# Attention and convolution on one core: the max tiles from 64 rows, in pairs on the two row halves, around the prob x val matmuls

## What is computed

```python
t = _gn(x).reshape(B, C, S).transpose(0, 2, 1)            # S = 1024 positions
q, k, v = t @ Wq.T + bq, t @ Wk.T + bk, t @ Wv.T + bv
q, k, v = (z.reshape(B * NUM_HEADS, S, hd) for z in (q, k, v))   # 8 heads, hd = 64
attn = softmax(einsum('gqd,gkd->gqk', q, k) / sqrt(hd))
wv = einsum('gqk,gkd->gqd', attn, v).reshape(B, S, NUM_HEADS, hd).transpose(0, 2, 3, 1)
x = x + wv.reshape(B, C, W, H)
x = x + conv3x3(relu(_gn(x) * mask(_gn(x))), weight) + bias
```

## Time and profile before

| | |
|---|---|
| median of 3 runs | 2684.11 us (2684.02 to 2684.46) |
| the profiled execution, own time | 2683.13 us |
| its span in the trace | 2681.2 us |
| granted TensorE clock, mean | 0.989 |
| TensorE matmul busy | 2560.5 us, 95%, 11424 instructions |
| VectorE busy | 2030.5 us, 76% |
| ScalarE busy | 1088.5 us, 41% |
| GpSimd busy | 1110.8 us, 41% |
| max tiles on TensorE (L646) | 1024, 388.3 us busy |
| their reductions on VectorE (L1186) | 1024, 661.0 us busy, 684 ns each |
| prob x val (L693) | 2048 records, 499.8 us busy |

### The profile page before, as it was taken

How to read it: one execution, slowest core, us unless ns; L and a number is a source line. 1 busy time by engine, 2 the same in 40 slices (tenths; PEclk the granted TensorE clock), 3 DMA queues, 4 the chain that set the end, 5 groups by cost and what they waited for, 6 DMA issues and landing times.

```text
span 2681.2 us, 38876 instructions
## 1 busy us (share of the span) xinstructions
PE 2560.5 (95%) x11424; PEld 1004.8 (37%) x11424; DVE 2030.5 (76%) x2804; ACT 1088.5 (41%) x1801; POOL 1110.8 (41%) x881
## 2 busy tenths in 40 slices
PE   5999999999999999999999999976999999999998
PEld 2333333333333333333333333322344444444443
DVE  5887787787788788778878877787468968968614
ACT  3455455445545545544554554443322132122100
POOL 3356466546556646655655564534103003003000
PEclk9999999999999999999999999988999999999999
DMA  5224142241423414323243331521254653744534
GB/s 150 80 74 114 61 130 82 61 133 48 123 81 95 112 40 130 100 66 110 61 118 93 92 94 33 152 84 58 90 209 169 221 203 126 275 149 142 188 109 158
DMA packets 209768, 309.01 MB, mean 115 GB/s; under 512 B 80272, under 2 KB 129552, under 8 KB 209552
## 3 DMA queue, kind: packets, MB, share of 16 engines
q1 hardware_dynamic: 209552, 306.36, 37.0%
HBM read 202.88 MB, written 52.69 MB: 95 GB/s over the span
## 4 chain that ended last, share of the span: by engine, by line
PE 83%; DVE 11%; issue 3%; ACT 1%; POOL 1%; DMA 0%; DVEq 0%; SPq 0%; ACTq 0%
PE bank L786 28%; PE bank L693 15%; PE bank L671 13%; PE bank L628 11%; PE bank L646 7%; PE bank L638 5%; DVE nmax L1186 3%; PE bank L660 2%; DVE prob_sum L1180 2%; PE bank L687 1%; ACT prob L869 1%; DVE nt L219 1%; DVE rstd L224 1%; PE bank L654 1%; DVE nt L221 1%
## 5 line engine op out<-in xcount | busy, mean ns | idle before, releaser
L1186 DVE TENSOR_REDUCE nmax<-bank 128x1 f32<-128x512 f32 x1024 | 661.0, 684 | 227.3 <-PE bank L646 213.1
L869 ACT ACTIVATE prob<-bank 128x512 f32<-128x512 f32 x1024 | 556.0, 596 | 653.5 <-PE bank L671 647.2
L786 PE MATMUL bank<-v,u_slab 128*128 128x512 f16 x3456 | 746.9, 379 | 0.0
L1026 POOL TENSOR_TENSOR prob_sum<-prob_sum,prob 128x512 f32<-128x512 f32 x360 | 526.0, 1461 | 419.4 <-ACT prob L869 417.9
L693 PE MATMUL bank<-prob,val 128*64 128x512 f32 x2048 | 499.8, 606 | 0.0
L786 PEld LDWEIGHTS bank<-v,u_slab 128*128 128x128 f16 x3456 | 338.2, 98 | 406.9 <-issue 0.8
L646 PE MATMUL bank<-k_a,q_a 128*128 128x512 f16 x1024 | 388.3, 385 | 27.4 <-DVE nmax L1186 22.0
L1180 DVE TENSOR_TENSOR prob_sum<-prob_sum,prob 128x512 f32<-128x512 f32 x360 | 358.9, 997 | 12.0 <-DVE shift L1196 8.9
L671 PE MATMUL bank<-q_a,k_a 128*128 128x512 f16 x1024 | 315.4, 382 | 17.7 <-ACT prob L869 16.0
L671 PE MATMUL bank<-q_b,k_b 128*128 128x512 f16 x1024 | 306.0, 381 | 2.4 <-DMA q_b<-shift 2.2
L1077 POOL TENSOR_TENSOR t_a<-tab_mem 128x1224 f32<-128x1224 f32 x16 | 49.2, 3073 | 460.6 <-DVEq L1309 446.9
(11 more groups left out here) (124 smaller groups left out, 2647.9 us busy)
## 6 DMA issues: line engine op xcount, KB each, us to landing
u_slab<-u_scratch SPq DMA_DIRECT2D x72, 1024.0 KB, 5.0
tile<-x_scratch SPq DMA_DIRECT2D x34, 1024.0 KB, 7.2
xs<-x SPq DMA_DIRECT2D x28, 1024.0 KB, 5.7
u_scratch<-u_w SPq DMA_DIRECT2D x96, 192.0 KB, 2.7
q_a<-qk_hi SPq DMA_DIRECT2D x64, 256.0 KB, 4.8
den_sb<-recip_scratch SPq DMA_DIRECT2D x128, 128.0 KB, 2.9
x_scratch<-xr SPq DMA_DIRECT2D x16, 1024.0 KB, 4.3
xr<-x SPq DMA_DIRECT2D x15, 1024.0 KB, 8.0
```

What stands on the lines that cost most here:

```text
L786: mm = pe.matmul(bank_at(pos, co)[:].rearrange("p (i n) -> p i n", i=2), slab[:, l, c, co * P:(co + 1) * P], image[v][:, 2 * c:2 * c + 2, ...
L869: act.activation(prob[:, (2 * u + e) % 8], sc_bank[bank_turn(s * 16 + 2 * u + e, 16 * HPI)[0]][:], ACT.Exp, scale=float(D) ** -0.5).then_i ...
L1026: nc.gpsimd.tensor_tensor(acc, in0, prob[:, (2 * kc + 1) % 8], ALU.add).then_inc(s1["sum1"], 1)
L1186: dve.tensor_reduce(nmax[:, m // 2, m % 2:m % 2 + 1], src[:], AX.X, ALU.max, negate=True)\
```

## The change

Each max tile is now made from the high halves alone, with a contraction over 64 rows: the even tiles from rows 0 to 63 of q_a and k_a, the odd ones from rows 64 to 127 of q_a and k_b. For that k high is put on rows 64 to 127 of k_b, q low on those of q_b, and the shift row and its 8.0 row are row 0 of q_b and k_b. The product of q high and k low is no longer part of the maximum (it stays in the scores). The tiles come in pairs of an even and an odd one: `MAX_PAIRS` = [2, 1, 2, 1, 2, 0, 0, 0]. In units 0, 2 and 4 one pair stands behind score part 1 and one behind `weigh_pair` (a new place, "e"), in units 1 and 3 one pair between the score parts. Place "a" is gone.

```diff
-MAX_QUOTA = [2, 3, 3, 3, 3, 2, 0, 0]
+MAX_PAIRS = [2, 1, 2, 1, 2, 0, 0, 0]
...
-    first = sum(MAX_QUOTA[:u])
-    tiles = [("max", first + k) for k in range(MAX_QUOTA[u])] if nxt else []
-    at = {"a": tiles[0:1], "b": tiles[1:2], "c": tiles[2:]}
+    first = 2 * sum(MAX_PAIRS[:u])
+    tiles = [("max", first + k) for k in range(2 * MAX_PAIRS[u])] if nxt else []
+    at = {"b": tiles, "c": []} if u % 2 else {"b": [], "c": tiles[0:2], "e": tiles[2:]}
...
-                hi_to = ((k_a, 0), (k_b, 0)) if which == 0 else ((q_a, 0), (q_a, D))
-                lo_to = (k_a, D) if which == 0 else (q_b, 0)
+                hi_to = ((k_a, 0), (k_b, D)) if which == 0 else ((q_a, 0), (q_a, D))
+                lo_to = (k_a, D) if which == 0 else (q_b, D)
...
-                sp.dma_start(q_b[half][D:D + 1, :, tok], shift[:, s % 2]).then_inc(s1["shift_row"], 16)
+                sp.dma_start(q_b[half][0:1, :, tok], shift[:, s % 2]).then_inc(s1["shift_row"], 16)
...
-                pe.matmul(dst[:].rearrange("p (k t) -> p k t", t=TOK), q_a[half][:, m // 2, tok],
-                          k_a[half][:, 4 * (m % 2):4 * (m % 2) + 4, tok],
+                k_hi, row = ((k_a, slice(0, D)), (k_b, slice(D, P)))[m % 2]
+                pe.matmul(dst[:].rearrange("p (k t) -> p k t", t=TOK), q_a[half][row, m // 2, tok],
+                          k_hi[half][row, 4 * (m % 2):4 * (m % 2) + 4, tok],
...
-                    run("a")
                     scores(h, s, u, 0)
                     run("b")
...
                     if u >= 2 and u % 2 == 0:
                         weigh_pair(h, s, u // 2 - 1, den_direct(s, more))
+                    run("e")
...
-                nc.gpsimd.memset(k_b[half][D:P], 0.0).then_inc(s1["kb_clear"], 1)
-                nc.gpsimd.memset(q_b[half][D:P], 0.0).then_inc(s1["kb_clear"], 1)
+                nc.gpsimd.memset(k_b[half][0:D], 0.0).then_inc(s1["kb_clear"], 1)
+                nc.gpsimd.memset(q_b[half][0:D], 0.0).then_inc(s1["kb_clear"], 1)
...
-                nc.gpsimd.memset(k_b[half][D:D + 1], 8.0).then_inc(s1["kb_clear"], 1)
+                nc.gpsimd.memset(k_b[half][0:1], 8.0).then_inc(s1["kb_clear"], 1)
...
-                    for place in "abcd":
+                    for place in "bcde":
```

More of the change, by code:

```diff
@@ L711, in run @@
                     def run(place):
-                        for kind, a in items[place]:
+                        for kind, a in items.get(place, ()):
                             if kind == "max":
```

## The result

The changed kernel takes **2771.18 us** (median of 4 runs, 2769.24 to 2774.72), the kernel before 2684.28 us beside it: a ratio of 1.032, 95% interval 1.0305 to 1.0336. That is 87 us slower. The forecast was 2704 us, 20 us slower, with a range up to 2745: the sign is right, the size is not, and the time lies outside the range.

What follows compares the result with a forecast made beforehand. PE (TensorE) was taken to bound the attention phase, so every step counts in full. Terms -104 + 60 + 48 + 12 + 16 - 11 = +21 us on a median of 2684.1 gave 2704 us, range 2650 to 2745.

Steps and rivals of the forecast that it cites:

- Tiles: Max tiles on PE: sixteen steps of 0.216 us become eight if halves fully overlap, -1.73 us a slot, -104 us.
- No overlap: Rival: the two halves of a pair do not run together, each pair takes 0.43 us; 2782 us, chance 0.07.
- Changes of shape: PE switching array shape around max pairs: five visits a slot at 0.20 us each, +1.0 us a slot, +60 us.
- The ring: Three banks hold max tiles; PE waits 0.4 us at each pair between score parts, +0.8 us a slot, +48 us.
- slots 0 and 1: In unit 3, extra VectorE work delays the bank for the pair between score parts: +0.87 us in 14 slots, +12 us.
- C pairs: Pairs between the two score parts of odd units, two a slot; each saves 0.22 us, pays 0.20 and 0.4.
- Slots 3 and 7: Without projections, fewer max tiles cover PE's wait for exp between units: +0.43 us twice and +0.22, +16 us in all.
- Waits that go: PE waits in slot 6 vanish, -0.9 us in 7 slots; slot 2 is 0.65 us better 7 times; -11 us together.
- The same DMAs are issued, at the same places of SP's queue: DMAs of the new layout: only their target rows change, so they cost nothing.
- Slots 60 to 62 at nothing: Last image's three late slots that still make max tiles are paced by others than PE; the change costs nothing there.
- The rule of the Trainium skill that I set against the change: Tiling speeds TensorE up, not the emptying of PSUM; reductions stay at 0.69 us, their cost counted in the ring term.
- The estimate of 2735 us from the Trainium skill: A pair takes longer than one step: 1.3 steps for a set, 0.065 us a pair, making it 2735 us.

Runs made afterwards that it cites:

- run 6: Changed kernel with its 64-row max tiles standing singly in the order of the kernel before: 2816.66 us, ratio 1.049.
- run 5: Changed kernel with one VectorE instruction moved, the reciprocal of unit 4 ahead of the reductions of the pair behind prob x val: 2749.24 us, ratio 1.0243.
- run 7: Changed kernel with the pair between the score parts put behind the second part, and the reciprocal moved as in run 5: 2716.7 us, ratio 1.0114.
- run 8: run 7 with unit 0's first pair ahead of the first score part and VectorE's moments last in units 1 and 2: 2688.21 us, ratio 1.0017.
- run 4: Changed kernel with the shift made one unit earlier, in unit 5 instead of 6: 2776.07 us, ratio 1.0347.
- run 2: Changed kernel's order with max tiles over all 128 rows instead of 64: 2752.56 us, ratio 1.0263.
- run 9: run 8 with the next slot's shift issued behind prob x val of unit 6 in slots 3 and 7: 2678.51 us, ratio 0.9974.
- run 10: run 9 with, in slot 2 alone, the pair ahead of unit 0's first score part moved to unit 5: 2678.85 us, ratio 0.9981.
- run 3: Changed kernel with the pair between the score parts put behind the second score part: 2740.86 us, ratio 1.0211.

## Why the prediction went wrong, step by step

- **Tiles, -104 us: right.** The halves overlap; the pair costs one step. "No overlap" (2782 us) came within 11 us of the measured time and was still wrong: a time alone does not tell the cases apart.
- **Changes of shape, +60: right.** 0.10 us each, 0.20 a visit (runs 6 and after). The plain slot has +0.14 where -1.73 + 1.0 + 0.8 gives +0.07.
- **The ring, +48, and slots 0 and 1, +12: right in kind; the total is nearly right partly by luck.** The second tiles of 126 C pairs start 72.9 us in all behind the first, 0.58 each, against 60 us by the prediction. For the two pairs of a slot together (images 1 to 5) it is 0.81 us in slot 5, where 0.8 was taken, and 1.17 in slots 0 and 1, where 1.67 was; but 1.48, 1.54 and 1.59 in slots 3, 6 and 7, where 0.8 was.
- **Slots 3 and 7, +16: right.** The wait between score parts 0 grew from 0.52 to 1.39 us there (by starts, per slot), +0.87, where 2 x 0.43 was worked out. What these slots lost beyond that is the ring's, 0.7 to 0.8 us a slot more than was taken.
- **Waits that go, -11: wrong.** In slot 6 the wait ahead of the sums' matmuls went, and the C pairs wait 0.7 us more than a plain slot was given. In slot 2 more went than I had taken (17 us for 4.6), and the wait for the row took over.
- **"The same DMAs are issued, at the same places of SP's queue": this is the step that failed.** I costed the DMAs at nothing. Their places are the same, but a queue in program order is as late as its first member, and that hangs on a reciprocal on VectorE, which the new place "e" pushed behind two reductions. I had looked at PE's own waits and at what VectorE does for the ring, and asked of nothing else on VectorE who waits for it; nor had I asked what the two tiles ahead of score part 1 of unit 0 had covered. What the runs showed in its place: PE's list has 33.6 us more at the row and 6.8 at the loop's turns, and in slots 0 to 58 the lower clock was granted nine times for 3.4 us (in six of the eight slots 2 and three times in slot 1), where it was once before; at 1.66 us each that is some 13 us. The three make 53 us, but they are not 53 of the 67 us between forecast and result, since in slot 2 they stand where PE had waited for VectorE. Putting the one reciprocal back returned 22 us (run 5), and 28 more went with the cover and the moved moments (runs 7 and 8). Runs 5 and 4 show the chain; that the cover is the larger part of run 8 is not shown, since its two edits were not run apart.
- **"Slots 60 to 62 at nothing": wrong.** Together they went from 123.2 to 130.7 us, nearly all of it in slot 61 (40.1 to 48.4). It comes with the order and not with the halves: slot 61 takes 49.3 us in run 2, full tiles in the new order, and 39.9 in run 6, halved tiles in the old one. Even run 9 has 47.2 there. Which wait it is was not looked for and stays open.
- The rule of the Trainium skill that I set against the change (TensorEngine Tiling (Array Packing), PSUM Bottleneck) points to the ring: it holds in kind, since the reductions became no shorter (682 ns each, 684 before). The estimate of 2735 us from the Trainium skill (TensorE: Matmul & The Clock Gate, Measured speedup vs the span model) has no support: a pair takes one step.

The range failed because all its cases varied terms that I had found. None was kept for a wait that the old order had hidden.

What the halves give directly is seen only where nothing waits. The plain slot had no idle time before and next to none in run 9; it takes 29.23 us there against 29.79, -0.56, where the terms give -0.63 (-1.73 and 1.0, and 0.10 for the change of shape that place "a" adds). An image takes 223.9 us in run 9 against 226.1 before; but image 0 is 2.2 us longer, so slots 0 to 59 are 12.3 us shorter in all, and slots 60 to 62 take 5.8 of that back (129.0 against 123.2). Full tiles in the order of run 9 were not run, so how much of its gain over the kernel before is due to the other moves is not shown.

## What to carry to other kernels

When work is moved on an engine that runs in program order, list everything queued behind it there, small instructions too, and follow each to the queue it feeds: here a reciprocal of 0.19 us started a chain of DMAs with a row at its end that TensorE needs. When filler is moved away, ask what it had been covering. And a saving on the bottleneck counts only with the waits around it: in the order of the change halving the tiles made the kernel slower by 19 us, and with the halved tiles in a mended order it is 0.15 to 0.36% faster than before.

## What was not expected of the hardware

**Small VectorE instructions stand still beside GpSimd.** In runs 5 and 7 to 10 PE waits 1.8 to 2.8 us in each slot 2 for VectorE, at max tiles. The instructions shown are part of the statistics of the next image, 128 x 4 numbers each. Run 8, VectorE, then GpSimd in the same time:

```profile
1037.88 1.20 DVE L216 TENSOR_SCALAR rstd<-nt 128x4 int32<-128x4 int32 x1
1039.11 1.18 DVE L219 TENSOR_TENSOR nt<-rstd 128x4 f32<-128x4 f32 x1
...
1041.19 1.20 DVE L224 SCALAR_TENSOR_TENSOR rstd<-nt,rstd 128x4 f32<-128x4 f32 x1
1042.42 0.16 DVE L219 TENSOR_TENSOR nt<-rstd 128x4 f32<-128x4 f32 x1
```

```profile
1037.78 1.27 POOL L1027 TENSOR_TENSOR prob_sum<-prob_sum,prob 128x512 f32<-128x512 f32 x1
1039.00 1.27 POOL L1040 TENSOR_TENSOR xr<-xr,den_sb 128x512 f32<-128x512 f32 x1
...
1041.10 1.27 POOL L1027 TENSOR_TENSOR prob_sum<-prob_sum,prob 128x512 f32<-128x512 f32 x1
```

The same instruction takes 0.16 us when GpSimd is still and 0.83 to 1.20 when it is not; each slow one shown starts just behind a GpSimd instruction and ends just behind that one's end. The chain of five such instructions costs about 5 us instead of 1. In the changed kernel the same lines took 0.16 to 0.17 us (1079.08 to 1080.04), because the late broadcasts held GpSimd idle until 1081.04; from 1081.06 on they took 0.83 to 1.26 us there too. In the kernel before five of them had taken 0.84 to 1.20 us, from 1036.62 on, and PE its 19.2 us of waits in the slots 2. So the cure of the row's wait gave part of itself back: GpSimd got its work earlier and stood in VectorE's way again. The Trainium skill has the rule (SBUF — State Buffer, "SBUF: two separate sides": VectorE and GpSimd share a pair of ports, and whoever holds it blocks the other for its whole instruction; it holds for a VectorE instruction in a two-port mode, or with two inputs in SBUF beside a GpSimd one that reads SBUF). The rows agree in that VectorE's instruction of 1039.11 ended at 1040.29, 0.02 us behind GpSimd's of 1039.00; which mode VectorE ran in they do not show. No run moved GpSimd's work alone, so the cause rests on the two timelines.

**A short wait can cost more than its length.** Behind 2.26 us of idle time the granted clock was 0.52 for 3.4 us, and eight passes took 3.55 us instead of 1.89; behind 1.69 us in run 3, 3.45. But the length of the wait alone does not decide it. In the changed kernel eight passes took 1.94 us behind 2.56 us of idle time (slot 2 of image 5) and behind 0.99 us (slot 4). In run 4 even the longest wait for the row was followed by passes at their usual length:

```profile
1091.22 0.60 PE L672 MATMUL bank<-q_b,k_b 128*128 128x512 f16 x2 [3.56 <-DMA q_b<-shift]
...
1092.08 1.94 PE L694 MATMUL bank<-prob,val 128*64 128x512 f32 x8
```

**The loop's turn costs more when a load has just been issued.** From PE's last projection to its next matmul it took 1.11, 2.47 and 0.74 us before, after the change and in run 5 (means of five turns), where the load of 1 MB had been issued 6.2, 4.7 and 7.1 us ahead of that projection. That it is a fetch of code that waits behind the data is argued from the packets of the instruction queues, which end 0.4 us ahead of PE's restart in the first two turns shown; in run 5 they end 1.5 us ahead of it, at the same turn. No run moved the load alone.
